# Attention block on one Trainium2 core: the low parts of the probabilities by whole units, in turn on VectorE and GpSimd

## The reference, cut to what matters

```
xn  = silu(group_norm(x, 32 groups) * scale + offset)
q, k, v = split(xn @ w_qkv)                  # 8 heads of 64 channels, 1024 positions
p   = softmax(q k^T / 8)                     # 1024 x 1024 for each head
out = (p v) @ w_out + b_out + x
```

## Time and profile before

| | |
|---|---|
| median of 3 runs | 3912.16 us (3911.99 to 3916.34) |
| the profiled execution | 3913.47 us, its span 3911.7 us |
| TensorE's granted clock, mean | 0.989 of full speed |
| busy share of the span | TensorE 93%, VectorE 86%, ScalarE 72%, GpSimd 45% |
| chain that ended last | TensorE 59%, VectorE 24%, issue 12%, ScalarE 3% |

### The profile page before, as it was taken

The page is one execution under the profiler, slowest core; times in us unless marked ns, Lnnn a source line. Parts: engine busy times, 40 slices in busy tenths (PEclk is TensorE's granted clock), DMA queues, the critical chain, the costliest instruction groups (busy, mean ns, idle before and its releaser), DMA issues.

```text
span 3911.7 us, 92342 instructions
## 1 busy us (share of the span) xinstructions
PE 3645.2 (93%) x32844; PEld 2099.9 (54%) x32844; DVE 3350.5 (86%) x4368; ACT 2812.9 (72%) x3074; POOL 1766.6 (45%) x1738
## 2 busy tenths in 40 slices
PE   3889999999999999999999999999999999999997
PEld 1455555555555555555555555555555555555553
DVE  5688888988898898988989888898988989888885
ACT  2577677777777777777777777777777777777774
POOL 1244444445445354444445444454444545444443
PEclk7999999999999999999999999999999999999999
DMA  2211212221121321212222121321212222131220
GB/s 77 56 44 51 76 39 66 55 74 52 45 82 34 88 55 45 82 39 66 55 69 58 44 80 36 87 55 45 79 42 66 55 69 58 39 84 37 62 59 33
DMA packets 120727, 228.89 MB, mean 59 GB/s; under 512 B 12624, under 2 KB 29008, under 8 KB 120272
## 3 DMA queue, kind: packets, MB, share of 16 engines
q1 hardware_dynamic: 120272, 222.87, 21.0%
HBM read 71.57 MB, written 33.55 MB: 27 GB/s over the span
## 4 chain that ended last, share of the span: by engine, by line
PE 59%; DVE 24%; issue 12%; ACT 3%; DVEq 1%; DMA 1%; POOL 0%; SPq 0%; ACTq 0%; POOLq 0%
PE SD L949 22%; PE PV L1081 11%; DVE mx L759 8%; PE ST L1051 8%; PE ST L1052 8%; PE TP L963 7%; DVE Pl L812 4%; DVE z L802 3%; DVE ms L729 2%; PE TP L970 2%; PE ST L1016 1%; DVE res L712 1%; PE ST L1023 1%; DVE st L773 1%; DVE OT L721 1%
## 5 line engine op out<-in xcount | busy, mean ns | idle before, releaser
L495 POOL TENSOR_TENSOR Pl<-P,Ph 128x512 f16<-128x512 f32 x1024 | 1240.1, 1211 | 1714.7 <-ACT Ph L608 1705.1
L605 ACT ACTIVATE P<-ST,cns 128x1024 f32<-128x1024 f32 x1024 | 1142.1, 1115 | 896.2 <-PE ST L1052 866.5
L759 DVE TENSOR_REDUCE mx<-TP 128x1 f32<-128x1024 f32 x1024 | 1246.4, 1217 | 165.2 <-PE TP L963 157.4
L608 ACT ACTIVATE Ph<-ST,cns 128x1024 f16<-128x1024 f32 x1024 | 1134.6, 1108 | 0.0
L812 DVE TENSOR_TENSOR Pl<-P,Ph 128x512 f16<-128x512 f32 x1024 | 978.8, 956 | 10.2 <-ACT Ph L608 6.1
L1081 PE MATMUL PV<-V,Ph 128*128 128x129 f16 (+2 forms) x10240 | 862.6, 210 | 4.4 <-POOL Pl L495 1.6
L1081 PEld LDWEIGHTS PV<-V,Ph 128*128 128x128 f16 x10240 | 772.3, 97 | 126.3 <-ACT pv_sum L616 9.2
L1081 PE MATMUL PV<-V,Pl 128*128 128x65 f16 x8192 | 835.2, 192 | 0.0
L1081 PEld LDWEIGHTS PV<-V,Pl 128*128 128x128 f16 x8192 | 723.2, 98 | 108.8 <-issue 0.8
L1051 PE MATMUL ST<-QK 128*128 128x512 f16 x2048 | 778.5, 380 | 0.2 <-ACT Ph L608 0.2
L1052 PE MATMUL ST<-QK 128*128 128x512 f16 x2048 | 778.1, 380 | 0.0
(11 more groups left out here) (96 smaller groups left out, 2849.6 us busy)
## 6 DMA issues: line engine op xcount, KB each, us to landing
QK<-QK SPq DMA_DIRECT2D x384, 256.0 KB, 4.7
res<-in_x SPq DMA_DIRECT2D x128, 256.0 KB, 2.8
out<-res SPq DMA_DIRECT2D x128, 256.0 KB, 2.0
x_in<-in_x SPq DMA_DIRECT2D x61, 512.0 KB, 3.8
V<-V SPq DMA_DIRECT2D x16, 1040.0 KB, 6.4
V<-in_L_conv_w_qkv SPq DMA_DIRECT2D x1, 3072.0 KB, 10.7
P<-in_L_conv_w_out SPq DMA_DIRECT2D x1, 1024.0 KB, 12.2
z<-in_x SPq DMA_DIRECT2D x1, 512.0 KB, 6.8
```

The costliest lines, as they stand in the source:

```text
L495: nc.gpsimd.tensor_tensor(Pl[:, v % 4, HALF:], P32[:, v % 2, HALF:], Ph[:, v % 4, HALF:], ALU.subtract).then_inc(lo_pool, 1)
L605: nc.scalar.activation(P32[:, v % 2, :], ST[:, slot, :], ACT.Exp, scale=cns[:, 0:1])
L608: nc.scalar.activation(Ph[:, v % 4, :], ST[:, slot, :], ACT.Exp, scale=cns[:, 0:1]).then_inc(exp_done, 1)
L759: nc.vector.reduce_max(mx[:, hh, qb:qb + 1], TP[:], AX.X).then_inc(top_drained, 1)
```

## The change

Unit by unit in turn, one engine makes the whole low part:

- Odd units: ScalarE writes `P32` and `Ph` as before, and GpSimd subtracts all 1024 columns in one instruction.
- Even units: ScalarE writes `Ph` first and then the 32-bit exponential in place over the scores in `ST` (PSUM); VectorE subtracts all 1024 columns from there. It does so in the odd unit behind, ahead of the low part of a turn. The slot of `ST` is free only then: what comes two places later in the ring waits for VectorE's subtraction (`lo_dve`) and no more for the exponential.
- `times_v` waits once, for the engine that had the unit.
- The tables move: xt turns 2 and 3 from (0,7), (0,9) to (0,5), (0,7), with their loads; ot turn 1 from (2,8) to (2,12); the statistics one at a time; all eight silu pieces now in odd units; their activations up to one unit earlier; the bias in even units.

```diff
-TURNS = {(0, 1): ("xt", 0), (0, 3): ("xt", 1), (0, 4): ("ot", 3), (0, 7): ("xt", 2), (0, 9): ("xt", 3),
-         (2, 0): ("ot", 0), (2, 8): ("ot", 1), (3, 4): ("ot", 2)}
+TURNS = {(0, 1): ("xt", 0), (0, 3): ("xt", 1), (0, 4): ("ot", 3), (0, 5): ("xt", 2), (0, 7): ("xt", 3),
+         (2, 0): ("ot", 0), (2, 12): ("ot", 1), (3, 4): ("ot", 2)}
...
-BN_AT = {(0, 5): (0, 2), (0, 7): (4, 6), (0, 11): (1, 3), (0, 13): (5, 7)}
+BN_AT = {(0, 5): (0,), (0, 6): (2,), (0, 7): (4,), (0, 8): (6,), (0, 9): (1,), (0, 10): (3,), (0, 12): (5,),
+         (0, 13): (7,)}
 AGGREGATE_AT, NEWTON_AT, COEF_AT = (0, 14), (1, 5), (1, 7)
-Z_AT = [(1, 8), (1, 11), (1, 13), (2, 1), (2, 4), (2, 7), (2, 11), (2, 13)]
-TANH_AT = [(1, 9), (1, 12), (1, 15), (2, 3), (2, 5), (2, 9), (2, 12), (2, 15)]
-SILU_AT = [(1, 11), (1, 13), (2, 0), (2, 4), (2, 7), (2, 11), (2, 13), (3, 0)]
-LOW_XN_AT = [(1, 12), (1, 14), (2, 1), (2, 5), (2, 8), (2, 12), (2, 14), (3, 1)]
-BIAS_AT = {(3, 0): 0, (3, 2): 1, (3, 5): 2, (3, 6): 3}
-LATE_BIAS_AT = {(1, 0): 4, (1, 2): 5, (1, 6): 6, (1, 8): 7}
+Z_AT = [(1, 7), (1, 9), (1, 12), (1, 15), (2, 3), (2, 5), (2, 8), (2, 11)]
+TANH_AT = [(1, 8), (1, 11), (1, 13), (2, 1), (2, 4), (2, 7), (2, 9), (2, 13)]
+SILU_AT = [(1, 9), (1, 13), (1, 15), (2, 3), (2, 5), (2, 9), (2, 11), (2, 15)]
+LOW_XN_AT = [(1, 10), (1, 14), (2, 0), (2, 4), (2, 6), (2, 10), (2, 12), (3, 0)]
+BIAS_AT = {(3, 2): 0, (3, 6): 1, (3, 8): 2, (3, 10): 3}
+LATE_BIAS_AT = {(1, 0): 4, (1, 2): 5, (1, 4): 6, (1, 6): 7}
...
-                nc.gpsimd.tensor_tensor(Pl[:, v % 4, HALF:], P32[:, v % 2, HALF:], Ph[:, v % 4, HALF:], ALU.subtract
+                nc.gpsimd.tensor_tensor(Pl[:, v % 4, :], P32[:, v // 2 % 2, :], Ph[:, v % 4, :], ALU.subtract
...
-                    if not (first and v == 0):
+                    if v % 2 == 0 and not (first and v == 0):
                         low_probs(b, v - 1)
...
-                nc.scalar.activation(P32[:, v % 2, :], ST[:, slot, :], ACT.Exp, scale=cns[:, 0:1])
+                if v % 2 == 1:
+
+                    wait(act, lo_pool, 32 * b + v // 2 - 1)
+                    nc.scalar.activation(P32[:, v // 2 % 2, :], ST[:, slot, :], ACT.Exp, scale=cns[:, 0:1])
 
                 wait(act, pv_done, UNITS * b + v - 3)
-                nc.scalar.activation(Ph[:, v % 4, :], ST[:, slot, :], ACT.Exp, scale=cns[:, 0:1]
-                                     ).then_inc(exp_done, 1)
+                exp_hi = nc.scalar.activation(Ph[:, v % 4, :], ST[:, slot, :], ACT.Exp, scale=cns[:, 0:1])
+                if v % 2 == 0:
+                    exp_hi = nc.scalar.activation(ST[:, slot, :], ST[:, slot, :], ACT.Exp, scale=cns[:, 0:1])
+                exp_hi.then_inc(exp_done, 1)
...
-                nc.vector.tensor_tensor(Pl[:, v % 4, 0:HALF], P32[:, v % 2, 0:HALF], Ph[:, v % 4, 0:HALF],
-                                        ALU.subtract).then_inc(lo_dve, 1)
+                nc.vector.tensor_tensor(Pl[:, v % 4, :], ST[:, slot, :], Ph[:, v % 4, :], ALU.subtract
+                                        ).then_inc(lo_dve, 1)
...
-                if at < 2:
-                    wait(pe, exp_done, UNITS * b - 1 + at)
-                    return
-                kind, n = ring[at - 2]
-                if kind == "score":
-                    pe.wait_ge(exp_done, UNITS * b + n + 1)
+                kind, n = ring[at - 2] if at >= 2 else ("score", at - 2)
+                if kind == "score" and n % 2 == 0:
+                    wait(pe, lo_dve, 32 * b + n // 2 + 1)
+                elif kind == "score":
+                    wait(pe, exp_done, UNITS * b + n + 1)
```

More of the change, by code:

```diff
@@ L388, in step @@
                             load_x(b + 1, 0)
-                        if u in (1, 3, 7):
-                            load_x(b + 1, (1, 3, 7).index(u) + 1)
+                        if u in (1, 3, 5):
+                            load_x(b + 1, (1, 3, 5).index(u) + 1)
                     if s == 0 and u == 4:
@@ L601, in exponentials @@
                 act.wait_ge(scores_ready, UNITS * b + v + 1)
-                wait(act, lo_dve, UNITS * b + v - 1)
-                wait(act, lo_pool, UNITS * b + v - 1)
-                nc.scalar.activation(P32[:, v % 2, :], ST[:, slot, :], ACT.Exp, scale=cns[:, 0:1])
+                if v % 2 == 1:
+                    wait(act, lo_pool, 32 * b + v // 2 - 1)
+                    nc.scalar.activation(P32[:, v // 2 % 2, :], ST[:, slot, :], ACT.Exp, scale=cns[:, 0:1])
                 wait(act, pv_done, UNITS * b + v - 3)
-                nc.scalar.activation(Ph[:, v % 4, :], ST[:, slot, :], ACT.Exp, scale=cns[:, 0:1]
-                                     ).then_inc(exp_done, 1)
+                exp_hi = nc.scalar.activation(Ph[:, v % 4, :], ST[:, slot, :], ACT.Exp, scale=cns[:, 0:1])
+                if v % 2 == 0:
+                    exp_hi = nc.scalar.activation(ST[:, slot, :], ST[:, slot, :], ACT.Exp, scale=cns[:, 0:1])
+                exp_hi.then_inc(exp_done, 1)
             def sums_out(b, half):
@@ L805, in silu, with low_probs @@
                 nc.vector.tensor_copy(xn[:, par, c, half, 0], z[:, i % 2]).then_inc(xn_hi, 1)
-            def low_probs(b, v):
+            def low_probs(b, v, slot):
                 dve.wait_ge(exp_done, UNITS * b + v + 1)
                 wait(dve, pv_done, UNITS * b + v - 3)
-                nc.vector.tensor_tensor(Pl[:, v % 4, 0:HALF], P32[:, v % 2, 0:HALF], Ph[:, v % 4, 0:HALF],
-                                        ALU.subtract).then_inc(lo_dve, 1)
+                nc.vector.tensor_tensor(Pl[:, v % 4, :], ST[:, slot, :], Ph[:, v % 4, :], ALU.subtract
+                                        ).then_inc(lo_dve, 1)
             def sums(b, half):
@@ L832, in step @@
                         side(use, image_of(use, b, s), cnt)
+                    if v % 2 == 1:
+                        low_probs(b, v - 1, even_slot)
                     for use, slot in turned:
                         low_output(use[1], image_of(use, b, s), slot)
-                    if not (first and v == 0):
-                        low_probs(b, v - 1)
                     if v % 4 == 3 and not (first and v == 3):
@@ L840, in step @@
                         top_use(use, b + 1, cnt)
-                    cnt.next_slot()
+                    if v % 2 == 0:
+                        even_slot = cnt.next_slot()
+                    else:
+                        cnt.next_slot()
                     turned = [(use, cnt.next_slot()) for use in unit_turn(s, u, first, last)]
@@ L934, in _ @@
                 step(B - 1, s, 1, now, last=True)
-            low_probs(B - 1, UNITS - 1)
             sums(B - 1, 15)
@@ L1059, in times_v @@
                 pe.wait_ge(exp_done, UNITS * b + v + 1)
+                pe.wait_ge(lo_pool if v % 2 else lo_dve, 32 * b + v // 2 + 1)
                 if kp == 0:
@@ L1067, in times_v @@
                 for i in range(2):
-                    pe.wait_ge(lo_pool if i else lo_dve, UNITS * b + v + 1)
                     kb = 2 * kp + i
```

## The result

The changed kernel takes 4143.27 us (median of 4 runs, 4140.07 to 4143.87) against 3913.01 us: 1.0585 of the time before, 95% interval 1.0567 to 1.0604. It is slower by 230 us; 4137 was forecast.

What follows compares the result with a forecast made beforehand. TensorE, busy 93%, bounds the kernel, so only its waits count: 28.3 us per image instead of 13.6, 14.7 more, 220 us over 15 images, plus 4 and 1 in the last: median 4137 us, range 3965 to 4195.

Steps and rivals of the forecast that it cites:

- slot behind ot turns: Scores behind four ot turns wait for VectorE's subtraction to free their slot: 1.35 us each, 5.4 us per image.
- slot behind xt turns: Xt turns wait for the even slot: 0.5 us for three, about 1.2 at (0,7); 2.7 us per image.
- held casts: Silu pieces in odd units: VectorE's cast waits out GpSimd's longer subtraction, delaying copies and drains; 11.9 us per image.
- coefficients: Behind (1,7), small operations meet GpSimd's subtraction; ScalarE's activation, then unit (1,8)'s drain come late; 3.6 us per image.
- mean and variance: Chains behind (0,15) and (1,3) are held by GpSimd's subtraction, then its bias sum: about 0.8 and 2.0, 2.8 us.
- the rest: Statistics in even units 0.9, activations moved ahead on ScalarE 1.0; loads, bias sums nothing: 1.9 us per image.
- VectorE's saved time: VectorE's PSUM subtraction saves 0.71 us per pair of units, 360 us busy; only TensorE's waits were counted as time.
- GpSimd's hold grows with its instruction: VectorE's SBUF instructions wait until GpSimd's ends, now 2.24 us in place of 1.16; both mechanisms in full: 0.64.
- The rival in which it does not grow: Waiting VectorE instructions are let in after at most 1.2 us: 18.1 us of waits per image, 3985 us; chance 0.13.
- The rival "faster": VectorE's casts and small operations get in ahead of GpSimd: 10.9 us of waits per image, 3876 us; chance 0.10.
- Turns hidden: Late drains absorb the turns' waits, or VectorE subtracts sooner: 8.1 us less per image, some 4010 us; chance 0.09.
- The step that failed: In units with shifts, lighter VectorE has `ms` ready before TensorE's shift, so all 13.6 us of present waits go.

Runs made afterwards that it cites:

- kernel 1: Changed kernel with GpSimd's whole-unit subtraction given as two instructions of 512 columns; 3995.38 us, ratio 1.0209.
- 12: Changed kernel with GpSimd subtracting only 768 of the 1024 columns of odd units, the other low parts left at zero; 4036.79 us, ratio 1.0315.
- kernel 6: Changed kernel with GpSimd subtracting only 32 of the 1024 columns of odd units, the other low parts left at zero; 3906.54 us, ratio 0.9982.
- kernel 2: Changed kernel with even units' 32-bit exponential in SBUF, so the score slot is free once the exponential is done; 4166.6 us, ratio 1.0648.
- kernel 9: Changed kernel with VectorE subtracting the low part ahead of the maximum in the four units with an ot turn; 4179.13 us, ratio 1.0677.
- kernel 11: Against kernel 8: GpSimd's low parts of silu one unit later, bias sum of (1,9) at (1,13); 3801.39 us, ratio 0.9710.
- kernel 10: Changed kernel with GpSimd's subtraction halved, casts behind the next drain, bias sums and silu low parts moved, first activation at (1,8); 3927.26 us, ratio 1.0033.
- 8: Kernel before with the new tables, casts behind the next drain, two bias sums moved, first piece's activation at (1,8); 3807.68 us, ratio 0.9730.

## Why the prediction was right

The forecast by its own terms, in us per image:

| term | forecast | measured | units |
|---|---|---|---|
| slot behind ot turns | 5.4 | 5.3 | (0,4), (2,0), (2,12), (3,4) |
| slot behind xt turns | 2.7 | 4.5 | (0,1), (0,3), (0,5), (0,7) |
| held casts | 11.9 | 9.1 | (1,10), (1,14), (2,4), (2,6), (2,10), (3,0) |
| coefficients | 3.6 | 3.5, of it 0.8 by the clock | (1,8), (1,9) |
| mean and variance | 2.8 | 4.8 | (0,15), (1,1), (1,3), (1,4) |
| the rest | 1.9 | 1.9 | |
| sum | 28.3 | 29.1 | |
| waits before | 13.6 | 14.0 | |

**Right.** That what TensorE waits for decides; that VectorE's saved time (126 us busy, as the held instructions gave back most of the 360) would not show; that GpSimd's hold grows with its instruction, which kernels 1, 12 and 6 show directly and which is all of the loss. The rival in which it does not grow (3985) is near kernel 1, whose hold is no longer than the one before (3995). The rival "faster" (3876) assumed no hold; with next to none kernel 6 takes 3907, 30 us more than that sum. "Turns hidden" was wrong: 5.3 us stand behind the ot turns.

**Sizes off.** Four terms, and their errors cancel, so that 4137 is nearer to 4143 than the working deserves: that closeness is luck. *Held casts,* 2.8 us too many: the price of (1,14) was taken for all four pieces with a shift's copy, and it measured 1.90 there but 1.58 to 1.65 at the other three; the two that delay the drain cost 1.2 and not 1.5; the two ahead of ot turns cost nothing beyond the turn (0.9 had been taken). In all of these the subtraction takes 2.13 us undisturbed, not 2.24. *Coefficients:* they ended 2.3 us into unit (1,8), with GpSimd's subtraction, and not at 3.2, so that the wait was 2.7 us and not 3.6. The fall of the clock behind it put 0.8 back; the working took TensorE's own time as fixed and had no term for that. *xt turns:* 0.54 at (0,3) and 1.11 at (0,7) as worked out, but 1.48 and 1.41 at the two with a shift. *Mean and variance:* 2.26 at (1,1) alone. These two have one cause.

One figure of the working is wrong without entering the sum: 13.6 us of waits in 235.3 are 5.8% of an image, not 3.5% of everything.

**The step that failed** is the sentence that `ms` would be ready ahead of TensorE's shift. It holds where nothing is late. In the undisturbed units of steps 1 to 3 `ms` starts 0.54 to 0.59 us before GpSimd's subtraction, and 0.32 before it at (0,9) and (0,13). Where VectorE is later than that in a unit with a shift, `ms` falls behind the start of GpSimd's subtraction and is held by it too, and then the price is the length of that subtraction and not the lateness. I priced lateness and hold as terms of a sum. Kernels 2 and 9 show that they are not: each takes about 1 us from the wait behind each ot turn, and 2.2 us come up at (2,13) and (3,5) in their place, because TensorE's waiting had kept `ms` ahead of GpSimd. By these waits alone kernel 2 breaks even and kernel 9 loses some 1.2 us per image; the rest of what they are slower than the changed kernel goes with the clock.

That VectorE's and GpSimd's instructions exclude each other for their whole length is what the Trainium skill states (SBUF — State Buffer, section "SBUF: two separate sides"); the four lengths of the cast agree. It names the two-operand and two-port instructions as those concerned: the trace is in keeping, with the cast and `ms` held, and the subtraction from PSUM at 1.21 in all its instances. That ScalarE writes PSUM faster than SBUF (ScalarE: Activation LUTs, section "Step-by-step: what each stage is for") agrees as well, by 0.02 to 0.03 us, which is worth nothing here.

**Left open.** Whether the new split could win was not settled. Not tried: ot turns elsewhere, and VectorE's whole units from SBUF together with the halves and the moves of kernel 11, which would take away both the slot waits and most of the hold. Kernels 6 and 10 leave the split 13 to 15 us of waits per image, 8 and 11 have 6 to 7. In kernel 10, 7.8 of the 15.1 us stand behind turns, 2.7 at mean and variance, 1.1 at (1,8), and the rest in small waits of at most 0.5.

## What to carry to other kernels

Where two engines exclude each other by instruction, the length of one instruction is a price of its own, apart from the busy time: twice as long and half as often costs every small operation that is late by a hair the whole of it. Cut long background instructions in pieces, and place short ones that others wait for where the other engine is known to be idle; here the move of one cast was worth 118 us. A wait on one engine may be what keeps another out of such a collision: before taking it away, ask what arrives next, and at which moment. And where TensorE bounds the kernel, read its granted clock behind the longest waits before two kernels are compared: here the falls of the clock were enough to turn the order of two of them.

## What the runs showed of the hardware

A held cast ended 0.28 to 0.29 us behind the recorded end of GpSimd's instruction at 512, 768 and 1024 columns alike, 0.15 us less than its own 0.43; a held `ms` ended 0.02 to 0.03 behind it, 0.20 less than its own 0.23. So the wait ends before GpSimd's recorded end, or a part of the held instruction runs during the wait; the records do not tell these apart. When two GpSimd instructions stand back to back and a VectorE instruction waits, VectorE gets in between (kernel 1, 1.27 and not 2.24 us). GpSimd's subtraction takes 1.16 us for 512 columns, 1.66 (mean) for 768 and 2.13 for 1024, so one whole instruction is 0.19 us cheaper than two halves, which is nothing beside what it holds up. The granted clock of TensorE fell to its lower level behind the wait at (1,8) in 1 of twelve images in the kernel before, 6 in the changed one and 12 in kernels 2 and 9; a fall in the changed kernel cost 1.3 to 1.7 us.
